# Four layers of graph attention on one core: compact inversion, shared rows of maxima, column masks on TensorE, and instruction lists by layer

## The reference

```python
# L0 (8 heads of 32): masked attention, then output projection, residual, layer norm
scores = einsum('bhqd,bhkd->bhqk', q, k) / sqrt(32)
scores = where(adj + eye > 0, scores, -inf)
x = layer_norm(x + softmax(scores) @ v @ Wo.T + bo)
# L1: scores += x@w_g[:D] (row) + x@w_g[D:] (column) + b_g + log(adj + 1e-9); x = softmax(scores) @ v + x
# L2 ("GAT", one head): logits = q_i + k_j, + (1-adj)*-1e9, leaky relu, softmax, times x@W_fc + b, + x
# L3: as L0 with scores + log(clip(adj, 1e-8)) in place of the mask
```

## Time and profile before

| | us |
|---|---|
| median of 3 runs | 2000.71 (1999.82 to 2002.35) |
| the profiled execution | 1996.07 |
| its span, first to last instruction | 1993.8 |
| busy: TensorE, DVE, POOL, ACT | 1805.7, 1659.6, 1235.7, 1223.2 |
| mean granted clock of TensorE | 0.969 of full speed |

### The profile page before, as it was taken

How to read it: one execution, slowest core, us unless ns; L and a number is a source line. 1 busy time by engine, 2 the same in 40 slices (tenths; PEclk the granted TensorE clock), 3 DMA queues, 4 the chain that set the end, 5 groups by cost and what they waited for, 6 DMA issues and landing times.

```text
span 1993.8 us, 54761 instructions
## 1 busy us (share of the span) xinstructions
PE 1805.7 (91%) x23693; PEld 1359.4 (68%) x23756; DVE 1659.6 (83%) x2656; ACT 1223.2 (61%) x1894; POOL 1235.7 (62%) x730
## 2 busy tenths in 40 slices
PE   5899998899999999889999999988999999987996
PEld 4666775677667677567766677657776677756774
DVE  4899887668899988767889989776889998877687
ACT  2566754457766675356766676535776677644575
POOL 3442776278954487527984458734896536872678
PEclk7999998999999999999999999999999999989998
DMA  5110010101220000000121000010021100001000
GB/s 148 34 33 12 18 34 12 33 12 44 65 61 27 12 18 28 22 22 18 60 65 54 13 17 18 23 43 7 28 65 54 44 18 18 19 21 38 12 28 33
DMA packets 67730, 66.44 MB, mean 33 GB/s; under 512 B 6050, under 2 KB 67492, under 8 KB 67492
## 3 DMA queue, kind: packets, MB, share of 16 engines
q1 hardware_dynamic: 67492, 62.95, 10.3%
HBM read 54.54 MB, written 8.39 MB: 32 GB/s over the span
## 4 chain that ended last, share of the span: by engine, by line
PE 54%; DVE 30%; ACT 9%; issue 4%; POOL 1%; SPq 1%; DMA 0%; DVEq 0%; POOLq 0%; ACTq 0%
PE gx L530 18%; PE sc L629 12%; PE od L664 11%; DVE rden L920 6%; DVE ring L915 5%; DVE qk L860 3%; PE gx L677 3%; DVE negm L881 3%; ACT aside L761 2%; ACT ring L776 2%; DVE negm L878 2%; PE gx L644 2%; PE sc L635 2%; PE sc L623 1%; DVE lg L954 1%
## 5 line engine op out<-in xcount | busy, mean ns | idle before, releaser
L515 POOL TENSOR_TENSOR ring<-ring,adj_c 128x1024 f32<-128x1024 f32 x256 | 608.6, 2403 | 157.5 <-ACT ring L774 90.3
L629 PE MATMUL sc<-qk 32*128 32x256 f32 x9216 | 418.2, 298 | 41.9 <-ACT aside L761 15.1
L629 PEld LDWEIGHTS sc<-qk 32*128 32x128 f32 x9216 | 330.4, 188 | 174.3 <-issue 137.7
L920 DVE RECIPROCAL rden<-od 128x256 f32<-128x256 f32 x192 | 335.7, 1748 | 6.3 <-PE od L664 6.3
L776 ACT ACTIVATE ring<-sc 128x1024 f32<-128x1024 f32 x256 | 248.5, 1024 | 67.3 <-PE sc L635 66.6
L520 POOL TENSOR_TENSOR xs<-xs,lr_g 128x512 f32<-128x512 f32 x64 | 82.7, 1293 | 322.4 <-ACT xs L783 322.4
L881 DVE TENSOR_REDUCE negm<-aside 128x4 f32<-128x1024 f32 x192 | 233.2, 1215 | 47.5 <-ACT aside L761 47.5
L878 DVE TENSOR_REDUCE negm<-sc 128x4 f32<-128x1024 f32 x192 | 234.1, 1219 | 33.3 <-PE sc L629 17.9
L664 PE MATMUL od<-ring,vf 128*32 128x256 f32 x3072 | 251.4, 400 | 1.3 <-POOL ring L515 1.3
L664 PE MATMUL od<-ring,ones_r 128*32 128x256 f32 x3072 | 240.6, 386 | 0.0
L761 ACT ACTIVATE aside<-sc 128x1024 f32<-128x1024 f32 x192 | 195.8, 1020 | 56.4 <-PE sc L635 28.5
(11 more groups left out here) (139 smaller groups left out, 4332.9 us busy)
## 6 DMA issues: line engine op xcount, KB each, us to landing
adj_c<-in_adj_t SPq DMA_DIRECT2D x96, 256.0 KB, 2.8
adj_r<-in_adj SPq DMA_DIRECT2D x64, 256.0 KB, 3.1
xs<-in_x SPq DMA_DIRECT2D x32, 256.0 KB, 2.8
out<-xs SPq DMA_DIRECT2D x32, 256.0 KB, 2.1
ring<-in_w_q SPq DMA_DIRECT2D x2, 256.0 KB, 5.7
ring<-in_w_k SPq DMA_DIRECT2D x2, 256.0 KB, 6.0
wo<-in_w_o SPq DMA_DIRECT2D x2, 256.0 KB
ring<-in_w_v SPq DMA_DIRECT2D x1, 256.0 KB, 3.8
```

Source lines behind the costliest of these rows:

```text
L515: pool.tensor_tensor(part, part, adj_c[i.mi % 3][:, t, :].unsqueeze(1).to_broadcast([P, G, N]), ALU.mult).then_inc(weighted, 1)
L629: mm = pe.matmul(sc[:, g, t * N:(t + 1) * N], buf[rows, a, c, t * P:(t + 1) * P], buf[rows, b, c, :], start=(n == 0 and not masked), stop= ...
L920: dve.reciprocal(rden[grp][:], od[grp][:, N:2 * N]).then_inc(rden_set, 1)
```

## The change

Four parts.

1. **Compact inversion.** Column blocks of the denominators are equal over 32 partitions. N's reciprocal of 128x256 becomes a DVE transpose in blocks of 32x32, a reciprocal of 128x8, and a transpose back from a broadcast of those eight columns.
2. **Shared rows of maxima.** `negp` packs both halves in one tile, so M is two matmuls instead of four and ACT's copy 128x256 instead of 128x512. E reads four rows (not two) with a stationary `pick` that is 1 in the rows of its own half. In L1, U takes five DVE instructions instead of seven.
3. **Column masks.** In L0, DVE's minimum is gone. POOL writes a bfloat16 `mask_c`, and E begins with four mask matmuls as S does. A waits for the exp alone.
4. **Lists by layer.** Each layer has its own table, with other places nearly everywhere. The weights' splits lie elsewhere in the first item. A fifth `fp` buffer is added and `dk` is kept in `lg`.

```diff
@@ tables (three of some hundred entries)
-    "A": {PE: [13.846, 14.231, 14.739, 15.739]},
+    "A": {PE: [13.457, 13.547, 15.008, 15.85]},     (MHA_PLAN0)
+    "A": {PE: [11.495, 12.869, 14.21, 14.607]},     (MHA_PLAN3)
@@ TensorE, S and E
+                            if i.l == 0:
+                                pe.wait_ge(mask_c_set, i.i0 + 1)
-                    masked = i.l == 0 and s == "S"
+                    masked = i.l == 0
                     if masked:
                         for g in range(G):
-                            pe.matmul(sc[:, g, :], ident_b[:], mask_r[i.i0 % 2][:].rearrange("p t n -> p (t n)"),
+                            pe.matmul(sc[:, g, :], ident_b[:], (mask_r if s == "S" else mask_c)[i.i0 % 2][:].rearrange("p t n -> p (t n)"),
@@ TensorE, M
-                    for n in range(C * T):
+                    for n in range(T):
                         mm = pe.matmul(gx_of("m", i)[:, n * P:(n + 1) * P], negp[i.mi % 2][:, n, :], ident_r[:],
@@ TensorE, A
-                        pe.wait_ge(masked_p, CH * i.i0 + c + 1)
+                        pe.wait_ge(exped, CH * i.mi + c + 1)
@@ POOL, PC in L0
-                        pool.tensor_scalar(buf[:], buf[:], 0.0, KEPT, ALU.is_gt, ALU.mult).then_inc(wt_set, 1)
+                        if i.i0 >= 2:
+                            pool.wait_ge(e_full, C * items_l0[i.i0 - 2].mi + C)
+                        pool.tensor_scalar(mask_c[i.i0 % 2][:], buf[:], 0.0, MASKED, ALU.is_le, ALU.mult)\
+                            .then_inc(mask_c_set, 1)
@@ DVE, E in L0
-                        dve.tensor_tensor(part, part, adj_c[i.mi % 3][:, t, :].unsqueeze(1).to_broadcast([P, G, N]), ALU.min)\
-                            .then_inc(masked_p, 1)
@@ DVE, N
-                    dve.reciprocal(rden[grp][:], od[grp][:, N:2 * N]).then_inc(rden_set, 1)
+                    dve.transpose(rden[grp][:], od[grp][:, N:2 * N]).then_inc(turned, 1)
+                    dve.wait_ge(turned, C * i.mi + grp + 1)
+                    dve.reciprocal(rden8[grp][:], rden[grp][:, 0:N:DH]).then_inc(inverted, 1)
+                    dve.wait_ge(inverted, C * i.mi + grp + 1)
+                    dve.transpose(rden[grp][:], rden8[grp][:].unsqueeze(2).to_broadcast([P, N // DH, DH])).then_inc(rden_set, 1)
@@ splits and rep
-            at.append((max(n - 4, -1) + 0.95, 0, n, engine, "I", items[0]))
+            at.append((-0.05 if n < 3 else 1.55 + (n - 3), 0, n, engine, "I", items[0]))
-                    if c == 2:
+                    if c == 3:
                         dve.wait_ge(w_plain, 16 * len(plain))
```

More of the change, by code:

```diff
@@ L22 @@
 NVF = 4
-NFP = 4
+NFP = 5
 NLG = 4
@@ L28 @@
 MASKED = -1e30
-KEPT = 1e38
 NEG_BIG = -1e9
@@ new lines @@
+MHA_PLAN3 = {
+    "T": {PE: [-1.19], ACTE: [-1.073], DVE: [-0.698]},
+    "Q": {PE: [0.636], ACTE: [0.369], DVE: [1.202]},
+    "P": {PE: [1.218], ACTE: [1.533], DVE: [2.181]},
+    "V": {PE: [5.67], ACTE: [6.124], DVE: [-9.553]},
+    "S": {PE: [3.514, 5.371], ACTE: [4.002, 5.553], DVE: [4.205, 5.767]},
+    "U": {DVE: [6.406]},
+    "M": {PE: [7.81], ACTE: [8.254]},
+    "E": {PE: [8.642, 10.048], ACTE: [8.758, 10.82], POOL: [7.379, 7.824]},
+    "A": {PE: [11.495, 12.869, 14.21, 14.607]},
+    "N": {DVE: [13.302, 15.208]},
+    "F": {PE: [19.244]},
+    "XB": {POOL: [-1.681]},
+    "H": {DVE: [19.215]},
+    "LC": {SP: [1.4]},
+    "PC": {POOL: [0.247]},
+}
@@ L64 @@
+LN_PLAN0 = {
+    "B": {DVE: [20.521]},
+    "Z": {ACTE: [21.887]},
+    "Y": {DVE: [27.099], ACTE: [28.749], POOL: [28.572]},
+}
+LN_PLAN3 = {
+    "B": {DVE: [19.777]},
+    "Z": {ACTE: [22.008]},
+    "Y": {DVE: [23.028], ACTE: [25.306], POOL: [23.757]},
 }
 FIRST_PLAN = {
-    "LX": {SP: [-6.376]},
-    "LR": {SP: [-4.102]},
-    "PR": {POOL: [-3.153]},
+    "LX": {SP: [-5.633]},
+    "LR": {SP: [-11.454]},
+    "PR": {POOL: [-3.015]},
 }
@@ L217, in gnn_stack @@
             in_order(("C", gats[n - NLG].k, 0), ("K", i.k, 0))
-        if n >= 2:
-            in_order(("K", gats[n - 2].k, 0), ("G", i.k, T - 1))
+            assert order[ACTE].index(("W", gats[n - NLG], 0)) < order[ACTE].index(("J", i, 0))
+    for engine in (PE, ACTE, DVE, POOL):
+        for group in ("T", "QP", "V", "S", "U", "M", "E", "A", "N", "F", "H", "B", "Z", "Y", "G", "J", "K", "L", "X", "W", "C", "XB", "PR", "PC"):
+            stages = (group,) if len(group) > 1 and group != "QP" else tuple(group)
+            run = [(i.k, stages.index(s), c) for s, i, c in order[engine] if s in stages]
+            assert run == sorted(run), (engine, group)
     with ExitStack() as ctx:
@@ L463, in _ @@
             pool.wait_ge(rows_set, ROW_STEPS)
+            flat_pick = pick[:].bitcast(F32)
+            pool.memset(flat_pick, 0.0).then_inc(pick_set, 1)
+            n = 1
+            for rows, h, value in ((2, 0, 1.0), (4, 1, 1.0), (2, 1, 0.0)):
+                for g in range(G):
+                    pool.wait_ge(pick_set, n)
+                    pool.memset(flat_pick[DH * g:DH * g + rows, h, :], value).then_inc(pick_set, 1)
+                    n += 1
+            pool.wait_ge(pick_set, PICK_STEPS)
             pool.wait_ge(w_first, 32)
```

169 lines of the change are left out of this document (88 added, 81 removed).

## The result

The changed kernel takes 1941.89 us (1935.82 to 1943.73) against 2001.13 us for the kernel before. The ratio is 0.9699, 95% interval 0.9677 to 0.9721: 3.0% faster. The forecast was 1967 us.

The account below looks back on a forecast made before the run. TensorE was taken as the bound, GAT as latency-bound. Work 456.5 plus idle 19.4 makes 475.9 us a group; four groups -34.6, start +2.5, end -1.5 sum to -33.6, giving 1967 us, range 1940 to 2000.

Parts of the forecast that it names:

- Idle time of a group: TensorE's idle time in a group of eight graphs, forecast to fall from 37.5 to 19.4 us.
- The rival of `sc`: Handing over of `sc` in L0 and L1 becomes the bound: slower, 2031 us at 1 us an item; chance 0.12.
- The rival of dear transposes: DVE's transposes in N cost far more than 424 ns: slower, 2031 us at 1748 ns; chance 0.03.
- the likeliest case: The main forecast of 1967 us, idle time 14 to 25 us a group, range 1945 to 1990; chance 0.68.
- the rival "more is won": GAT's ends close up too and idle falls to 12 us a group: 1938 us; chance 0.10.
- the ledger: TensorE's work in a group: 447.1 us, plus 14.9 for masks, minus 5.5 for M, makes 456.5 us.
- the most that new lists and a free DVE can give back is 37.5 us a group: TensorE's idle time over L0, L1, GAT and L3, 37.5 of 484.55 us, taken as the limit of gain.
- I book nothing for it by itself: Compact inversion in N: 1.3 us an item saved on DVE, hidden beneath TensorE wherever DVE is not full.
- The start: Constants and seven weights load ahead of the first graph: first S0 at about 40 us, +2.5 us (0 to +8).
- The tail: Program's end: two inversions of the last item in line, each 0.65 us shorter, booked at -1.5 us.

Follow-up runs that it names:

- the moved U: Changed kernel with L1's U ahead of N0 on DVE and POOL's first GAT product one attention product earlier: 1916.18 us, ratio 0.9583.
- the run with pieces: Changed kernel with POOL's products of 128x1024 written as four of 128x256, same order: 1965.88 us, ratio 0.9836.

## Why the forecast came out as it did

**Right, in part by luck.** Idle time of a group, 20.0 us for 19.4, though spread otherwise: L0 0.1 (forecast 3), L1 3.4 (3.5), GAT 12.3 (10.5), L3 4.3 (2.4). The sum came out by luck: 8.8 us of it are M's two waits behind POOL's products, which the forecast does not have, and without them 11.2 us would be left. The transposes, 443 and 446 ns for 420, so that N's inversion takes 1.2 us for 1.1. The masks, 0.85 us for 0.93. L0's item, 19.27 us for 19.4, and GAT's, 6.01 for 5.9. That the masks lose by themselves. The rival of `sc` did not come: a steady item of L0 has TensorE busy for all of its 19.27 us. The rival of dear transposes fell with 443 ns. The time, 1941.9 us, is below the 1945 to 1990 of the likeliest case and near the 1938 of the rival "more is won", but not by that rival's mechanism, since idle time did not fall to 12 us.

**The step that failed** is the ledger itself: "TensorE's work of a group is then 447.1 + 14.9 - 5.5 = 456.5 us". It measured 446.9, 9.6 us less (445.7 in the second group). The second group of the changed kernel, in stretches that begin and end as in the earlier trace rows (L0, L1, GAT, L3), shows where:

```profile
506.48:660.12 153.64, 151.90 (x1910) 104.78 (x1912) 97.91 (x209) 101.69 (x146) 87.27 (x62) 1.00 0.16 48
660.12:792.38 132.26, 127.74 (x1962) 99.38 (x1964) 104.08 (x219) 91.46 (x140) 94.11 (x53) 0.99 0.06 18
792.38:883.45 91.07, 75.34 (x748) 60.55 (x740) 68.14 (x133) 42.89 (x94) 41.07 (x23) 0.96 0.09 24
883.45:974.13 90.68, 90.68 (x1350) 70.51 (x1343) 72.66 (x144) 67.91 (x99) 78.67 (x42) 1.00 0.13 40
```

In L0 the ledger holds: 142.44 + 11.2 - 1.8 = 151.8 us of work, and 151.9 were measured. In L1 it says 134.1, and 127.7 were measured. For GAT and L3 together it says 170.6, and 166.0 were measured. The masks were 13.6 for 14.9: 1.3 us. M saved up to 0.44 us an item where TensorE sets the pace, which in all 24 would be 10.6 us for 5.5: at most 5.1 us. In L0 such a saving does not show, for the ledger holds there with cheaper masks. The other 3.2 us or more are what remains, and by my reading had been no work: time that the records of before give to matmuls that stood in a wait or ran at the lower clock, while the step took all 447.1 us of busy time as work that stays. That such time exists is shown by the moved U, which took 5.4 us of idle and 2.4 of busy time off one stretch. How the 8.3 us divide between M and such time is not shown. So "the most that new lists and a free DVE can give back is 37.5 us a group" was no bound either.

**The second one** is "I book nothing for it by itself" of the inversion. It gives 5.7 us a group alone, and it is what makes the lists possible. I gave the lists the whole gain. Alone they cost 17.5 us a group; the three code parts alone give 6.8 (12.3 in the second group); together they give 17.8. The parts are not addends, and a sum by parts could be right only by luck. The forecast's mechanism, TensorE bound and its stops what is to be won, held. Its assignment to the parts did not.

**The start** was sized wrongly: +2.5 us (0 to 8) against 7.7 at the first scores and 6.7 more while filling in. I had counted TensorE's work behind the loads and had overlooked that the first transposes now wait for DVE's copy of the identity, and that this copy stands behind the split of `w_q`. **The tail** (-1.5) gave nothing that can be seen: the last group is 16.7 us shorter, as the others are 17 to 18.

By groups, 17.8 + 16.9 + 16.7 us in the last three and 2.7 in the first make the 54.1 us between the two profiled spans.

## What to carry to other kernels

Busy time of the bounding engine is not its work: take out what it does between waits, or better, price an edit by doubling it. When a schedule and the durations it was made for change together, test them apart before crediting either, for here the schedule without its code was 3.5% slower and the code without its schedule 2.3% faster. And look at where the small instructions of one engine fall in time against the long ones of another that shares its way to SBUF.

## What the runs showed of the hardware

Some of DVE's instructions stand still while POOL runs one of its own. DVE's `tensor_scalar`, cast and `tensor_tensor` on small SBUF tiles (128x2 to 128x16, 0.17 to 0.29 us alone) lasted up to 2.38 us beside POOL's products of 2.39 us, each ending just behind one of them. DVE's work with an operand in PSUM kept its duration (L982 0.68 to 0.69 us over 96 instructions), and so did the SBUF to SBUF transposes (0.444 to 0.448 over 192), reciprocals of 128x8, the maxima of `aside` (1.205 to 1.222) and even the `tensor_scalar` of 128x1 in the layer norm (L996, 0.20 to 0.22 over 128). The Trainium skill (SBUF — State Buffer, section "SBUF: two separate sides") says that DVE and GpSimd share a pair of ports under an exclusive lock for whole instructions, for DVE's two-port modes or two SBUF inputs. The durations here agree on DVE's side; that POOL waits for DVE is not shown by any run here. The end of one of POOL's instructions does not always let DVE in: in the run with pieces a cast stood through twelve of them (8.27 us).
